# Differential attention: the roots of Q's and K's sums move behind the later scores' exponential of their slot

## The reference, cut to what matters

```python
q, k = (_rms_norm(q), _rms_norm(k))          # x * rsqrt(mean(x * x) + eps), per head of 8 columns
q, k = (_apply_rotary(q, cos, sin), _apply_rotary(k, cos, sin))
y1 = _causal_attn(q1, k1, v, scale)          # softmax(q k^T * scale, causal) v, 8 heads
y2 = _causal_attn(q2, k2, v, scale)          # and 8 more
y = (y1 - lambda_full * y2).reshape(B, T, D)
return y @ Wproj.T
```

## Time and profile before

| | us |
|---|---|
| median of 3 runs | 3165.83 |
| lowest, highest | 3156.24, 3166.15 |
| the profiled execution, its time | 3165.76 |
| its span, first to last instruction | 3164.0 |
| mean granted clock | 0.954 of full speed |

### The profile page before, as it was taken

The page is one execution under the profiler, slowest core; times in us unless marked ns, Lnnn a source line. Parts: engine busy times, 40 slices in busy tenths (PEclk is TensorE's granted clock), DMA queues, the critical chain, the costliest instruction groups (busy, mean ns, idle before and its releaser), DMA issues. The chain is left out here.

```text
span 3164.0 us, 66212 instructions
## 1 busy us (share of the span) xinstructions
PE 2882.8 (91%) x22258; PEld 1871.3 (59%) x22258; DVE 2482.6 (78%) x6944; ACT 2326.2 (74%) x3601; POOL 2104.2 (67%) x2402
## 2 busy tenths in 40 slices
PE   6999997788998888789579999999999999999979
PEld 3555554344444444678246666666666666666668
DVE  5777776788888875567468888888888888888867
ACT  5888883466666667444289999999999999999833
POOL 5666673346555543577657888788877888788745
PEclk8999997799999999899789999999999999999989
DMA  4544534223322330685400000000000000000001
GB/s 121 131 108 112 129 92 91 59 62 69 69 57 60 72 70 19 191 271 158 128 1 1 17 1 17 1 7 11 6 12 1 17 1 17 1 17 1 1 14 41
DMA packets 151509, 178.31 MB, mean 56 GB/s; under 512 B 18619, under 2 KB 122784, under 8 KB 151076
## 3 DMA queue, kind: packets, MB, share of 16 engines
q1 hardware_dynamic: 142084, 157.14, 19.2%
q0 software_dynamic: 9088, 16.94, 1.6%
HBM read 99.82 MB, written 75.95 MB: 56 GB/s over the span
## 5 line engine op out<-in xcount | busy, mean ns | idle before, releaser
L3380 PE MATMUL lb_FF<-lb_h,lb_w 128*128 128x512 f32 x1024 | 502.0, 592 | 0.0
L3609 DVE TENSOR_SCALAR lb_z<-lb_M,lb_mv,lb_rstd 128x128 f32<-128x128 f32 x1024 | 344.9, 398 | 3.3 <-POOL lb_rstd L3534 3.0
L3497 ACT ACTIVATE lb_h<-lb_H,lb_prm 128x512 f32<-128x512 f32 x512 | 327.5, 699 | 2.6 <-PE lb_H L3371 2.6
L3534 POOL TENSOR_TENSOR lb_rstd<-lb_rstd,half 128x4 f32<-128x4 f32 x256 | 260.8, 1019 | 37.2 <-issue 1.3
L3365 PE MATMUL lb_H<-lb_x1s,lb_w 128*128 128x512 f32 x512 | 273.0, 533 | 0.0
L3380 PEld LDWEIGHTS lb_FF<-lb_h,lb_w 128*128 128x128 f32 x1024 | 193.5, 189 | 89.9 <-issue 61.1
L3601 DVE BATCH_NORM_STATS2 lb_stats<-lb_M 128x6 f32<-128x128 f32 x1024 | 226.9, 284 | 15.5 <-PE lb_M L3324 9.0
L1649 POOL TENSOR_SCALAR_AFFINE_SELECT da_PT<-da_PT 128x1024 f32<-128x1024 f32 x128 | 149.1, 1165 | 133.4 <-ACT da_PT L1566 133.3
L3366 PE MATMUL lb_H<-lb_x1s,lb_w 128*128 128x512 f32 x512 | 203.3, 397 | 0.0
L3371 PE MATMUL lb_H<-lb_x1s,lb_w 128*128 128x512 f32 x512 | 202.7, 397 | 0.1
L3552 POOL CAST lb_x1s<-lb_x 128x512 fp32r<-128x512 f32 x128 | 78.3, 611 | 173.7 <-DVE lb_x L3634 173.7
(11 more groups left out here) (514 smaller groups left out, 8860.8 us busy)
## 6 DMA issues: line engine op xcount, KB each, us to landing
moe_w<-experts_dram SPq DMA_DIRECT2D x39, 384.0 KB, 3.2
da_qT<-da_stq SPq DMA_DIRECT2D x64, 192.0 KB, 4.1
da_kT<-da_stk SPq DMA_DIRECT2D x64, 192.0 KB, 3.8
moe_x<-moe_xs SPq DMA_DIRECT2D x39, 260.0 KB, 3.6
tc_g<-moe_ys SPq DMA_DIRECT2D x32, 256.0 KB, 3.5
ga_q<-ga_stq SPq DMA_DIRECT2D x20, 384.0 KB, 5.8
lb_split<-moe_parts SPq DMA_DIRECT2D x8, 896.0 KB, 6.4
da_stq<-da_parts SPq DMA_DIRECT2D x16, 384.0 KB, 2.4
```

The lines of the kernel that those rows point to most:

```text
L3380: pe.matmul(FF[:, :], w2[:, k, :], h[:, k, :], start=(k == 0), stop=(k == KC - 1)).then_inc(ff_filled, 1)
L3497: act.activation(h[:, k, :], H[:, k % 2, :], ACT.Gelu_apprx_tanh, bias=col(FB1 + k, i)).then_inc(h_ready, 1)
L3534: pool.tensor_tensor(out[:, :], out[:, :], C["half"][:, 0:NT], ALU.pow).then_inc(done, 1)
L3609: last = v.tensor_scalar(z[:, t, :], M[:, t * P:(t + 1) * P], mv[:, t, 0:1], rstd[:, t:t + 1], ALU.subtract, ALU.mult)
```

## The change

In ACT's program the call of `exp_later(n)` moves up, ahead of the two calls of `rms`. Everything else of the loop keeps its order.

```diff
                     if m == 7 and next_but_one:
                         square(c2, K)
+                    if n < 8 * NB:
+                        exp_later(n)
                     if m == 1 and then:
                         rms(c, Q)
                     if m == 2 and then:
                         rms(c, K)
-                    if n < 8 * NB:
-                        exp_later(n)
                     if m == 3 and then:
                         copy_v(c)
```

## The result

| | before | changed |
|---|---|---|
| median of 10 runs, us | 3162.52 | 3171.77 |
| lowest, highest, us | 3156.24, 3166.15 | 3165.76, 3178.88 |
| the profiled execution, its time and span, us | 3165.76, 3164.0 | 3178.88, 3177.2 |

The ratio is 1.0033, with a 95% interval of 1.0022 to 1.0044. The kernel is slower, by 9.3 us in the medians. The forecast was nearly 8 us faster; the figure lies where rival (b) had put it, 3167 to 3175. All ratios are the recorded ones, not quotients of the two medians, from which they differ by up to 0.0011. Three slow executions of the variants (3378.84 us with the held mask, 3732.47 and 5613.95 with the same wait in the kernel before) are left out of every median and ratio.

A forecast was written before the change was run, and what follows sets the result against it. PE was taken to set the pace, ACT next. Seven batches at 0.35 (2.5), six at 0.35 + 0.39 (4.4) and about 1 for the first made 7.9: 3165.76 to 3157.9 us; 8-in-10 range 3141 to 3173.

The forecast's parts named there:

- rival (b): Fourth L1731 on DVE blocked by POOL's mask of m = 5, about 0.84 us; 3167 to 3175; chance 0.25.
- ACT and PE: L1571 ahead of the roots on ACT gives PE 1.38 us of lead by slot m = 4.
- DVE and POOL up to the copy: Q's split on DVE starts 0.96 us late; blocking with POOL decides the copy of O, 202.8 to 203.25.
- The middle value of 10.9: DVE's copy of O put at 203.0, between 202.8 and 203.25: 0.35 us earlier than before.
- the choice at the fourth L1731: On DVE, from the copy through the four L1731 to `turn_x`, the forecast kept 5.45 us: `turn_x` 0.35 us ahead.
- the stated limit: Mask of m = 5 blocks the fourth L1731 if it arrives less than 4.31 us behind the copy.
- The clock: PE's clock falls in six of 13 batches, 0.78 us each, behind slot m = 2's idle 1.49; half vanish.
- Rival (a): PE's whole lead reaches `turn_x`, 1.82 us ahead: 3136, or 3150 with half; chance 0.20.
- "right": Signs: L1416's wait about 13 us, `turn_x`'s 12 or more, L1298 waits, copy at 10.7 to 11.2, batches 29.0.
- PE's own pace: PE alone, from L1416 of m = 4 at 202.07, would reach `turn_x` at 206.98.

The follow-up runs named there:

- the held mask: Changed kernel plus one wait: POOL's mask of slot m = 5 waits until the fourth L1731 is done; 3151.08 us, ratio 0.9975.
- the same wait in the kernel before: Kernel before, with POOL's mask of slot m = 5 made to wait for the fourth L1731; 3163.56 us, ratio 1.0003.
- The two experiments that take the collision out and put it in: Mask of m = 5 held until fourth L1731, changed kernel: 0.9975; mask of m = 3 repeated behind that of m = 4, kernel before: 1.0047.

## Why the prediction failed, point by point

- **ACT and PE: right.** L1416 of m = 2, 3 and 4 was put at 2.85, 6.40 and 9.95 us of the batch and came at 2.86, 6.40 and 9.94. L1754 of Q was put 0.96 us late and was 1.00.
- **DVE and POOL up to the copy: right in kind.** The second cast of Q and the mask of m = 2 did come up together, and the mask won; that case had been worked out to a copy at 203.25, 11.13 us into the batch, and it came at 11.09. The middle value of 10.9 was 0.2 us too good: the forecast's 203.0 has to be 203.2.
- **The step that failed is the choice at the fourth L1731.** The forecast let it slip through ahead of the mask of m = 5, as before, and so kept 5.45 us from the copy to `turn_x`; that stretch measured 6.33 (143.56 to 149.89). The blocked L1731 was a term put at nothing in the forecast and at 0.84 in rival (b). The prediction had the mask arriving 4.25 us or somewhat more behind the copy's start, and let it decide at 4.31. The changed kernel's mask of m = 5, in the batch of the rows above, started at 147.91, which is 4.35 us behind the copy (143.56). It came later than the stated limit, and won all the same. These are the two instructions, each alone:

```profile
147.85 1.24 DVE L1731 TENSOR_SCALAR da_xn<-XT,da_mv,da_rstd 128x128 f32<-128x128 f32 x1
```

```profile
147.91 1.09 POOL L1649 TENSOR_SCALAR_AFFINE_SELECT da_PT<-da_PT 128x1024 f32<-128x1024 f32 x1
```

  The mask has its full speed, 1.09 us, and L1731, though it stands 0.06 us earlier in the trace, needs 1.24 instead of 0.34. DVE's rows overlap, so the start of an L1731 lies before the end of the one ahead of it (146.80 and 1.12 make 147.92). The pair stands like this, 0.06 to 0.07 us apart, in all thirteen batches. What counted, as far as these rows tell, was that the mask was there at 147.91 when the third one ended, not which of the two starts first in the trace; no run moves the mask by a few hundredths to test it. The Trainium skill's sentence (SBUF — State Buffer, Who interferes with whom) that the first to issue gets the pair can't be read off the starts alone here. The third one ended 4.36 us behind the copy. The kernel before would have shown that this end is later than 4.31, the end of the mask, on which the prediction let the race hang:

```profile
206.62 1.12 DVE L1731 TENSOR_SCALAR da_xn<-XT,da_mv,da_rstd 128x128 f32<-128x128 f32 x1
```

  It is the third L1731 of the earlier trace rows and ends at 207.74, 4.39 us behind the copy at 203.35. Against that limit the prediction's own arrival (4.25 or somewhat more) leaves the mask some 0.1 us to win by, and even against 4.31 it did not speak for the forecast: rival (b) should have had more than 0.25, and not half the chance of the forecast.
- **Rival (b) was right**, in place, price and sum: 0.84 us for a blocked L1731, measured 0.89; `turn_x` 0.49 later than before, measured 0.74 (the copy was the late one); 3167 to 3175, measured 3171.8. That the figure lies inside is in part luck: (b) added 0.7 to 8.7 us to a start of 3165.8, and measured are 9.3 us above 3162.5, since the first median, of three runs, was 3.3 us above that of ten. The two experiments that take the collision out and put it in bear it out. It was also systematic, in every batch, since the mask and L1731 both hang on the same copy: a race that looks even is decided once and then repeats 13 times.
- **The clock: wrong in kind.** I let half of the falls vanish because their idle 1.49 us at slot m = 2 went. They did leave that place, but the idle time was handed on to `turn_x` (1.58 us in one piece), and the fall came there, with 1.4 us for each instead of 0.78. Rival (b) had this term wrong too. Before, PE had waits in slots m = 3 to m = 5 that could take up part of a fall; behind `turn_x` it has hardly any (this reason is argued from the rows, not tested). The term was put at 2.3 us of gain and measured 2.3 of loss.
- **Rival (a) did not happen in the change**, but the DVE chain that it blamed was the right place: with the copy first and two masks held, `turn_x` comes at 15.13 and the time is 3137, where (a) in full had been put at 3136.

Of the signs, the wait of L1416 (9.4 us), that of `turn_x` (26.5), the new one of L1298 and the copy (11.09) came as "right" had them; the batches of 30.1 and the long fourth L1731 came as (b) had them. Of the small sums, PE's own pace adds up to 207.00 and not 206.98 (202.07 + 4.93), on which nothing hangs.

## What to carry to other kernels

When a wait is taken off one engine, ask which event the others now hang on together: here the copy released both PE (and through it a mask on POOL) and DVE's own chain, and the two met at the same instruction in every batch. Price such a meeting both ways, each as if it came in every batch, take as its limit the end of the instruction ahead of the one at stake, and look for a wait of one line that decides it. And a moved instruction has no worth of its own: the same move cost 9 us, brought 32 with DVE's order fitted to it, and that new order, with its two held masks but without the move, cost 10.

## What the runs showed of the hardware that I had not expected

- An instruction of DVE that starts earlier in the trace can still be held up for the whole length of one of POOL, when its predecessor had not ended (147.85 against 147.91, 1.24 against 0.34 us; the same in all thirteen batches).
- Where the idle time lay decided where the granted clock fell: at slot m = 2 before, behind `turn_x` in the changed kernel, in slot m = 4 with one mask held. With the copy first and no mask held, PE had an idle piece of 1.83 us at `turn_x` and the clock fell to 1.2 GHz in 10 of 13 batches. With one mask held and the same work that piece was 1.04 us, the clock stayed at 2.4 GHz in all 13, and `turn_x` came 0.8 us earlier. The two kernels differ by 22.6 us (3169.4 and 3146.8); the earlier `turn_x` makes 13 x 0.8 = 10.4 and the falls (30.84 against 29.40 each) 10 x 1.44 = 14.4, together 24.8.
- The length of the longest idle piece does not settle it either. In the changed kernel with one mask held, the clock fell in 3 of 13 batches right behind waits of 0.47 and 0.77 us (in one of the three 0.47 and 1.14) with 1.2 us between them, while the piece of 1.04 us just named never brought a fall. What decides between these was not tested.
